# A cross-attention and feed-forward kernel: spectra moved to POOL, rounding moved to ACT, and a new order around the second norm

## What is computed

```python
def attention(queries, keys, values, Wq, bq, Wk, bk, Wv, bv, Wo, bo):
    q, k, v = queries @ Wq.T + bq, keys @ Wk.T + bk, values @ Wv.T + bv       # 16 heads of 16
    corr = irfft(rfft(q) * conj(rfft(k)), n=512).mean(axis=-1)
    weights, delays = top_k(corr, 6)
    w = softmax(weights)
    out = (w * v_shifted_by(delays)).sum()
    return out @ Wo.T + bo

def act_quant(x):
    scale = 127.0 / clip(max(abs(x), axis=-1), 1e-05)
    return clip(round(x * scale), -128.0, 127.0) / scale

def bitlinear(x, w, b):
    return act_quant(rmsnorm(x)) @ weight_quant(w).T + b

x = x + attention(layernorm(x), ctx, ctx, Wq, bq, Wk, bk, Wv, bv, Wo, bo)
h = gelu(bitlinear(layernorm(x), w1, b1))
x = x + bitlinear(h, w2, b2)
```

## Time and profile before

| | |
|---|---|
| median of 3 runs | 181.99 us (181.75 to 182.73) |
| profiled execution, time | 182.84 us |
| profiled execution, span from the first to the last instruction | 180.8 us |
| PE busy | 159.7 us, 88% |
| DVE busy | 149.8 us, 83% |
| ACT busy | 89.7 us, 50% |
| POOL busy | 83.9 us, 46% |
| mean granted TensorE clock | 0.980 |

### The profile page before, as it was taken

The page is one execution under the profiler, slowest core; times in us unless marked ns, Lnnn a source line. Parts: engine busy times, 40 slices in busy tenths (PEclk is TensorE's granted clock), DMA queues, the critical chain, the costliest instruction groups (busy, mean ns, idle before and its releaser), DMA issues.

```text
span 180.8 us, 2886 instructions
## 1 busy us (share of the span) xinstructions
PE 159.7 (88%) x869; PEld 107.1 (59%) x877; DVE 149.8 (83%) x347; ACT 89.7 (50%) x158; POOL 83.9 (46%) x150
## 2 busy tenths in 40 slices
PE   7989889998999998999994977993799999999943
PEld 2635667657655956576873755670456766555632
DVE  1537299999299996999979999779997999999992
ACT  3136615548722441211510521519449999999821
POOL 6030899754440003932009827071985654454430
PEclk9999999999999999999999999999589999999999
DMA  5999989080474000000000001616447101111012
GB/s 191 319 289 391 359 289 190 3 116 0 64 107 61 5 0 0 0 0 5 2 0 0 0 0 29 91 29 87 64 59 115 58 29 58 44 45 62 29 58 87
DMA packets 14128, 15.07 MB, mean 83 GB/s; under 512 B 1186, under 2 KB 13347, under 8 KB 14116
## 3 DMA queue, kind: packets, MB, share of 16 engines
q1 hardware_dynamic: 9892, 10.73, 17.9%
q0 software_dynamic: 4224, 4.19, 15.8%
HBM read 8.61 MB, written 2.10 MB: 59 GB/s over the span
## 4 chain that ended last, share of the span: by engine, by line
PE 25%; DVE 24%; issue 7%; POOL 1%; DVEq 1%; ACT 0%; POOLq 0%
PE psum L469 4%; PE psum L458 4%; DVE c_f L1046 4%; PE psum L518 4%; PE psum L538 3%; DVE res L1061 2%; DVE hmax L1035 2%; DVE stats L910 2%; PE psum L520 2%; PE psum L338 2%; PE psum L529 2%; DVE prod_sum L763 1%; DVE xmax L924 1%; DVE m_b L884 1%; DVE out_f L891 1%
## 5 line engine op out<-in xcount | busy, mean ns | idle before, releaser
L390 PE MATMUL psum<-wkv,c_f 128*128 128x512 f32 x64 | 29.0, 598 | 0.8 <-ACT c_f L580 0.8
L1035 DVE TENSOR_REDUCE hmax<-wf 128x1 f32<-128x1025 f32 x16 | 19.4, 1211 | 0.7 <-ACT wf L683 0.7
L390 PEld LDWEIGHTS psum<-wkv,c_f 128*128 128x128 f32 x64 | 11.8, 190 | 13.7 <-issue 12.4
L683 ACT ACTIVATE wf<-psum,xdeq 128x1024 f32<-128x1024 f32 x16 | 17.6, 1101 | 1.3 <-PE psum L520 1.3
L599 ACT COPY kv_f<-psum 128x512 f32<-128x512 f32 x16 | 9.1, 582 | 18.4 <-PE psum L390 18.4
L691 ACT ACTIVATE x_f<-wf 128x1024 f32<-128x1024 f32 x16 | 16.9, 1056 | 0.0
L458 PE MATMUL psum<-to_signal,out_f 128*128 128x256 f32 x64 | 14.6, 382 | 2.4 <-POOL out_f L1170 2.4
L518 PE MATMUL psum<-w1q,xq_t 128*128 128x512 bf16 x59 | 16.2, 392 | 0.5 <-issue 0.3
L538 PE MATMUL psum<-w2q,kv_f 128*128 128x256 bf16 x128 | 16.4, 273 | 0.0
L469 PE MATMUL psum<-wo,out_t 128*128 128x256 f32 x64 | 14.9, 386 | 1.3 <-DVE out_t L898 1.3
L403 PE MATMUL psum<-wq,x_f 128*128 128x256 f32 x64 | 15.1, 381 | 0.8 <-ACT x_f L580 0.8
(11 more groups left out here) (164 smaller groups left out, 351.0 us busy)
## 6 DMA issues: line engine op xcount, KB each, us to landing
ctx_in<-in_ctx SPq DMA_DIRECT2D x4, 512.0 KB, 5.1
res<-in_x SPq DMA_DIRECT2D x4, 512.0 KB, 6.5
res<-bo_all POOLq DMA_DIRECT2D x4, 512.0 KB, 5.2
res<-b_all POOLq DMA_DIRECT2D x4, 512.0 KB, 5.9
out<-res SPq DMA_DIRECT2D x16, 128.0 KB, 1.7
wf<-in_w_t SPq DMA_DIRECT2D x1, 1024.0 KB, 8.3
wf<-in_w_t SPq DMA_DIRECT2D x2, 512.0 KB, 9.7
wkv<-in_wkv_t SPq DMA_DIRECT2D x1, 512.0 KB, 7.5
```

Of the source, the lines that this page charges most:

```text
L390: mm = pe.matmul(bank(K_BANKS + ft), c_f[:, c, ft * P:(ft + 1) * P], wkv[:, c, :], start=(c == 0), stop=(c == NC - 1))
L683: act.activation(hid[j], hb, ACT.Gelu, scale=xdeq[:, m, j:j + 1]).then_inc(s["hid_made"], 1)
L1035: dve.tensor_reduce(hmax[:, j:j + 1], hid_and_least[j], AX.X, ALU.max, apply_absolute_value=True).then_inc(s["hmax_made"], 1)
```

## The change

- `out_f` gets two buffers. POOL makes both parts of the spectrum for batches 0, 1 and 3 (`out_spectrum`); for batch 1 it waits for all cross spectra, for batch 3 for DVE's spectrum of batch 2. DVE makes batch 2 alone, in two halves of 128 columns (`out_spectrum_halves`), and `inverse(2, c)` waits for each half.
- `weigh` takes one step over two inputs where there were two (a comparison, then a product with sum), and the division by the sum moves into `turn_g`, which multiplies by a diagonal matrix in place of transposing by the identity.
- `turn_g(1)` and its copy stand between the halves of inverse(1), and four products of zeros are gone.
- Rounding of x to int16 moves from DVE to ACT (`round_x`); DVE makes its scale (`x_scales`) and the bf16 copy (`whole_x`).
- PE runs inverse(3) ahead of turn_x(0) and up(0, 0) ahead of project(3); turn_x(1) follows project(3), and turn_x(3) stands behind up(0, 3).
- DVE, ACT and POOL get orders of calls to match.

```diff
+FIRST_LATE = NB // NG
+TAKEN = -3.4e38
...
-        out_f = sb("out_f", [P, 2, 2, D])
+        out_f = sb("out_f", [P, 2, 2, 2, D])
+        m_halves = ctx_in[:].rearrange("p n (k f) d -> p (n k) f d", k=2)
...
                 for a in range(NA):
-                    mm = pe.transpose(psum[:, G_BANKS[g], a * GR:(a + 1) * GR], chosen[:, a * P:(a + 1) * P], eye[0:GR, 0:GR])
+                    mm = pe.matmul(psum[:, G_BANKS[g], a * GR:(a + 1) * GR], chosen[:, a * P:(a + 1) * P], g_diag[:],
+                                   start=True, stop=True)
...
             def inverse(n, c):
-                if c == 0:
-                    pe.wait_ge(s["out_re_made"], n + 1)
-                    pe.wait_ge(s["out_im_made"], n + 1)
+                if n == FIRST_LATE:
+                    pe.wait_ge(s["out_half_made"], 2 * c + 2)
+                elif c == 0:
+                    pe.wait_ge(s["out_re_made"], by_pool(n))
+                    pe.wait_ge(s["out_im_made"], by_pool(n))
...
             inverse(1, 0)
+            turn_g(1)
             inverse(1, 1)
-            turn_g(1)
-            keep_busy(X_BANKS, 4)
             spectrum_g(1)
             project(1, 0)
             project(1, 1)
+            inverse(2, 0)
+            inverse(2, 1)
+            keep_busy(X_BANKS, 5)
+            project(2, 0)
+            project(2, 1)
             pe.wait_ge(s["consts"], 3)
-            for n in (2, 3):
-                inverse(n, 0)
-                inverse(n, 1)
-                keep_busy(M_BANKS[1], 5)
-                project(n, 0)
-                project(n, 1)
-                turn_x(n - 2)
...
             pe.wait_ge(s["w_quantised"], 2)
             pe.wait_ge(s["b1_made"], 16 * NPART)
+            inverse(3, 0)
+            inverse(3, 1)
+            turn_x(0)
+            up(0, 0)
+            project(3, 0)
+            project(3, 1)
+            turn_x(1)
...
                     if t == 2:
                         keep_busy(T_BANKS + 1, 9)
                         turn_h(0, TURNED)
+                    if t == 3:
                         turn_x(3)
...
+            def round_x(n):
+                act.wait_ge(s["xscale_made"], n + 1)
+                if n:
+                    act.wait_ge(s["xq_made"], n)
+                for a in range(NA):
+                    ins = act.activation(xround[:, a, :], xc[:, n % 2, a, :], ACT.Identity, scale=xscale[:, a:a + 1])
+                ins.then_inc(s["xround"], 1)
...
             inverse_copy(1, 0)
+            copy_g(1)
             inverse_copy(1, 1)
-            copy_g(1)
             centre(0)
             inverse_copy(2, 0)
             inverse_copy(2, 1)
             centre(1)
-            copy_x(0)
+            round_x(0)
             inverse_copy(3, 0)
             inverse_copy(3, 1)
+            copy_x(0)
             centre(2)
-            copy_x(1)
+            round_x(1)
...
                     if t == 0:
+                        copy_x(1)
+                        round_x(2)
+                        square(0, 0)
                         centre(3)
                     if t == 1:
                         copy_x(2)
-                    square(m, j)
-                    if t == 2:
+                        square(0, 1)
+                        round_x(3)
+                    if t > 1:
+                        square(m, j)
+                    if t == 3:
                         copy_x(3)
...
-                dve.tensor_tensor(rest[:, 0:L], corr[:, 0:L], rest[:, 0:L], ALU.not_equal).then_inc(s["mask_made"], 1)
...
-                dve.tensor_tensor_reduce(out=expd[:], in0=expd[:], in1=rest[:, 0:L], scale=1.0, scalar=0.0,
-                                         op0=ALU.mult, op1=ALU.add, accum_out=gsum[:]).then_inc(s["gsum_made"], 1)
+                dve.scalar_tensor_tensor(chosen[:], rest[:, 0:L], TAKEN, expd[:], ALU.is_le, ALU.mult,
+                                         accum_out=gsum[:]).then_inc(s["gsum_made"], 1)
...
-                dve.tensor_scalar(chosen[:], expd[:], grec[:, 0:1], None, ALU.mult).then_inc(s["g_made"], 1)
+                dve.tensor_scalar(g_diag[:], eye[0:GR, 0:GR], grec[:, 0:1], None, ALU.mult).then_inc(s["g_made"], 1)
...
+            def out_spectrum_halves(n):
+                dve.wait_ge(s["g_ready"], n // (NB // NG) * 3 + 3)
+                dve.wait_ge(s["at_done"], n * 4 - 6)
...
+                for c in range(NC):
+                    h = slice(c * H // NC, (c + 1) * H // NC)
+                    cols = slice(c * P, (c + 1) * P)
+                    dve.tensor_tensor(m[0][:, :, h], v[0][:, :, h], g_r[:, :, h], ALU.mult)
+                    dve.tensor_tensor(m[1][:, :, h], v[1][:, :, h], g_i[:, :, h], ALU.mult).then_inc(s["m_half_made"], 1)
+                    dve.tensor_tensor(m[2][:, :, h], v[1][:, :, h], g_x[:, :, h], ALU.mult)
+                    dve.tensor_tensor(m[3][:, :, h], v[0][:, :, h], g_i[:, :, h], ALU.mult).then_inc(s["m_half_made"], 1)
+                    dve.wait_ge(s["m_half_made"], 2 * c + 1)
+                    dve.tensor_tensor(out_f[:, n % 2, :, 0, cols], m_halves[:, 0, :, cols], m_halves[:, 1, :, cols],
+                                      ALU.subtract).then_inc(s["out_half_made"], 1)
+                    dve.wait_ge(s["m_half_made"], 2 * c + 2)
+                    dve.tensor_tensor(out_f[:, n % 2, :, 1, cols], m_halves[:, 2, :, cols], m_halves[:, 3, :, cols],
+                                      ALU.add).then_inc(s["out_half_made"], 1)
...
+            def x_scales(n):
...
+                dve.tensor_scalar(xscale[:], xinv[:], -127.0, None, ALU.mult).then_inc(s["xscale_made"], 1)
...
-                    ins = dve.tensor_scalar(xround[:, a, :], xc[:, n % 2, a, :], xinv[:, a:a + 1], -127.0, ALU.mult, ALU.mult)
-                ins.then_inc(s["xround"], 1)
+            def whole_x(n):
                 dve.wait_ge(s["xround"], n + 1)
...
+            out_spectrum_halves(FIRST_LATE)
             stats2(0)
             mean_var2(0)
...
+            add_residual(1, 0)
+            add_residual(1, 1)
+            inverse_out(2, 0)
+            inverse_out(2, 1)
+            stats2(1)
+            mean_var2(1)
+            row_max(0)
+            x_scales(0)
+            add_residual(2, 0)
+            add_residual(2, 1)
+            x_deq(0)
+            whole_x(0)
+            row_max(1)
+            x_scales(1)
+            inverse_out(3, 0)
+            inverse_out(3, 1)
+            stats2(2)
+            mean_var2(2)
+            x_deq(1)
+            whole_x(1)
             row_max(2)
+            x_scales(2)
...
                     hidden_max(m, j)
+                    if t == 0:
+                        add_residual(3, 0)
+                        add_residual(3, 1)
+                        x_deq(2)
...
+                    if t == 0:
+                        stats2(3)
+                        mean_var2(3)
+                        whole_x(2)
+                    if t == 1:
                         row_max(3)
+                        x_scales(3)
                         x_deq(3)
+                    if t == 2:
+                        whole_x(3)
...
+            def out_spectrum(n):
+                if n != 1:
+                    pool.wait_ge(s["g_ready"], n // (NB // NG) * 3 + 3)
...
+                pool.tensor_tensor(by_heads(m_a[:]), v_of(n, 0), g_of(g_re, n), ALU.mult)
+                pool.tensor_tensor(by_heads(m_b[:]), v_of(n, 1), g_of(g_im, n), ALU.mult).then_inc(s["m_ab"], 1)
                 pool.tensor_tensor(by_heads(m_c[:]), v_of(n, 1), g_of(g_rx, n), ALU.mult)
                 pool.tensor_tensor(by_heads(m_d[:]), v_of(n, 0), g_of(g_im, n), ALU.mult).then_inc(s["m_cd"], 1)
...
-            for n in (0, 1):
-                out_im_products(n)
-                out_im(n)
-            out_im_products(2)
-            out_im(2)
+            out_spectrum(0)
+            pool.wait_ge(s["cross_made"], 4 * NG)
+            out_spectrum(1)
+            pool.wait_ge(s["out_half_made"], 2 * NC)
+            out_spectrum(3)
             x_rms(0)
-            out_im_products(3)
-            out_im(3)
             aug_parts(0)
...
+            h_deq(0, 0)
             x_rms(3)
-            h_deq(0, 0)
+            h_deq(0, 1)
             aug_parts(3)
             add_b2(3)
```

105 lines of the change are left out of this document (31 added, 74 removed).

## The result

The changed kernel takes **188.47 us** (median of 4 runs, 187.44 to 189.07), the kernel before on the same chip 182.36: ratio 1.0335, interval 1.0294 to 1.0375. (A ratio leaves out executions more than 1.5% above the fastest of the same kernel; medians and ranges hold all.) The forecast was 188.6, made as 181.99 and 6.6 more; the measured difference is 6.1. The profiled execution of the changed kernel took 187.44, its fastest; its span is 185.3.

The account below looks back on a forecast made before the run. DVE's entry into the steady feed-forward part was taken to set the time. Chain 5.1 plus clock 1.5 made 6.6 later, so 181.99 + 6.6 = 188.6 us; the forecast's own range was 187.4 to 190, the overall range 184.8 to 190.4.

Parts of the forecast that it names:

- The bound: Feed-forward part from its fourth tile: DVE sets the pace, so kernel time is DVE's entry there plus a constant.
- Up to g of the second group: Spectra, weigh and turn_g(1) up to the second group's g: ready at 95.2 against 94.5, between 0.3 and 1.2 late.
- the charge of 0.45 to POOL: POOL's batch 1 spectrum beside the new weigh at 86.6: contention for SBUF costs POOL 0.45 us.
- The chain: From second group's g to first finish: queues form one serial chain through ACT's rounding; finish at 144.4, 5.1 us later.
- Rival 3: Shorter hand-overs: three roundings on the chain at 1.14 instead of 1.65 (-1.5), no lower clock (-1.5): 185.6; chance 0.14.
- The clock term: PE idle 4 to 6 us before 139.3, so lower clock: turn_x +0.6, turn_h +0.45, down(0) +0.45; together +1.5, bounds 0 and 1.95.
- Rival 4: PE's clock stays up because its idle stretch is shorter than counted, all else as forecast: 187.1; chance 0.12.
- Rival 1: DVE's relief from rounding and spectra comes through, 4.5 us less after late g: faster, 177.5; chance 0.08.

Follow-up runs that it names:

- the last experiment: Against the 180.84 us kernel (new spectra, old order, clock kept, inverse(3) early): batch 2's rounding put on ACT, PE's products of zeros moved into idle time; 179.25 us.

## Why the prediction was right

**The bound.** Right. From the first `finish` to the end it is 41.5 us in both kernels, so the time is set by when DVE gets there.

**Up to g of the second group.** Forecast 95.2. DVE's last step of it is at 94.03 (its copy of `g_re` begins at 93.18), with the front 0.93 earlier in this execution, so the term is 0.2 too large. The diagonal products of turn_g(1) cost 0.64 more (1.07 against 0.43) and not 0.45. The part that failed is the charge of 0.45 to POOL for meeting `weigh`:

```profile
85.80 1.52 DVE L873 SCALAR_TENSOR_TENSOR chosen<-rest,expd 32x512 f32<-32x512 f32 x1
```

```profile
84.30 1.26 POOL L1201 TENSOR_TENSOR out_f<-m_a,m_b 128x512 f32<-128x512 f32 x1
85.53 1.26 POOL L1203 TENSOR_TENSOR out_f<-m_c,m_d 128x512 f32<-128x512 f32 x1
```

POOL's two sums take 1.26 each, with and without the meeting. DVE's step took 1.52, where the same step for the first group, with POOL idle, took 0.68. POOL was first and lost nothing; DVE, second, paid. This is what the Trainium skill, "SBUF — State Buffer", section "SBUF: two separate sides", says of the exclusive lock. My 0.45 came from rows 3, and I had read them without the row ahead of them in the kernel before:

```profile
94.53 0.69 DVE L883 TENSOR_TENSOR m_a<-kv_f,g_re 128x512 f32<-128x512 f32 x1
```

DVE's `m_a` at 94.53 stood ahead of POOL's `m_c` at 94.58, so there POOL was second and took 1.56 in place of 1.06; `m_b`, from 95.14, then came second to POOL. The extra 0.5 was the price of coming second, and I had charged it to the one that came first. POOL's products are 1.06 throughout, as forecast.

**The chain.** Right in every link. Forecast less measured time: project(2) 104.6 and 103.48, 1.1; end of inverse_out(3) 113.0 and 111.77, 1.2; whole_x(1) 118.2 and 116.95, 1.25; hidden_max(1) 129.1 and 127.44, 1.7; hidden_max(2) 136.2 and 134.43, 1.8. Of this 0.93 is the front, and 0.7 grew on the way through rounded-up hand-overs. The waits that I had named were 3.0, 2.5 and 2.4 on ACT and are 2.98, 2.27 and 2.36; that in front of `finish` was 4.0 in my list and is 5.27, since it holds the lower clock too. `round_x` takes 1.69; I had chosen the row of ACT's centring (1.71) over DVE's 1.14. Rival 3 rested on the other end and fell with it.

**The clock term.** Right in its place, and near in size: turn_x(3) to turn_h(1) 1.46 (0.87 + 0.6 forecast), turn_h(1) to its copy 1.07 (0.65 + 0.45), and `down` in a stretch where the clock came back (0.84 on average):

```profile
142.00:145.00 3.00, 3.00 (x23) 1.85 (x22) 1.13 (x3) 2.31 (x4) 0.92 (x3) 0.84 0.02 5
```

I had charged 1.5. With zeros ahead of turn_x(3) DVE's wait shrank by 1.2 and the kernel's median fell by 1.8. Rival 4 (the clock stays up) gave 187.1.

**What the forecast had not.** The gap of 2.1 us ahead of project(2), which I had written down in passing ("the inverse of batch 2 had been ready at 101. Project(2) starts at 104.6") and not read as idle time of PE. In some executions it costs 1.7. That the median came out at 188.47 for a forecast of 188.6 is partly luck: the profiled execution alone, forecast at 189.4, took 187.44, with 0.93 of the 2.0 from the front and most of the rest from the 0.2 and the 0.7 above. The median is 1.0 above that execution, and where this 1.0 lies stays open, as no slower execution of the changed kernel was profiled. A fall of the clock ahead of project(2) would cost 1.7, a late front up to 1.5, and the profiled execution has one of the earliest fronts, 70.69. The mean granted clocks of its four executions don't favour the first: 0.963 at 187.44 us and 0.973 at 189.07. The forecast had neither of the two.

**Rival 1**, that the relief of DVE comes through, named a real gain: DVE is busy 136.6 us instead of 149.8, 13 less, and all of it turned into waits: its idle time in the span grew by 18. Waits that stay small came about in the last experiment, at 179.25. The Trainium skill, "Perfetto Trace Analysis", section "Optimizing Scalar/DVE Operations", says that moving work from a saturated DVE to the scalar engine may pay. In this case both answers were measured: with all four roundings on ACT and DVE standing in the copy, it costs 4.0 (188.47 against 184.43); with one, under a tile of DVE's other work, DVE is relieved of 0.97 us and doesn't wait, and the kernel, whose zeros were moved as well, is the fastest of all.
